# An expert layer on Trainium2: GpSimd's gathers and scatters, from a loop with copied indices to written-out code

## The chip, the core and the metric

The kernel runs on one core of one Trainium2 chip. The metric is device time in microseconds (us); of the kernel before there are three runs, with a median of 521.87 us (520.72 to 522.24). One more execution was recorded by the hardware profiler; all durations below come from it.

## The reference, cut to what matters

4096 tokens of 192 channels (16 images of 16 x 16) go through a convolution block, an attention block and an expert block. Only the expert block is touched:

```
t = t + ffn(layernorm(t))
ffn(x):
    logits = einsum('btd,ed->bte', x, gate_w)         # 8 experts
    p, idx = top_k(softmax(logits), 2)                # 2 experts for each token
    p = p / (sum(p) + 1e-8)
    h = silu(x @ gate_bank[e]) * (x @ up_bank[e])     # 192 -> 384
    y = h @ down_bank[e]                              # 384 -> 192
    return sum over the two chosen e of p[e] * y[e]
```

The kernel computes only the chosen experts.

## The kernel before, in words

Four phases follow one another, each a block of programs, one for each engine, with a barrier between blocks: convolution, attention, routing and experts. Routing sorts the 8192 pairs of a token and an expert by expert, and cuts them into 72 tiles of 128 rows, so that a tile has one expert. It leaves `idx_map` in on-chip memory: for each tile and each of 128 partitions two integers, the token's row to be gathered (entry 0) and the row to be scattered to (entry 1). `tile_exp` holds each tile's expert. VectorE writes both, in the routing block.

In the expert block (`expert_phase`, from L1023), the engines work on the tiles 0 to 71 in one order:

- GpSimd starts the indirect transfers. `gather` (L1057) brings a tile's 128 rows of `rows` (256 channels and 8 gates) from device memory into `xt`, a ring of XR = 8 slots. `scatter` (L1067) writes a tile's results from `y`, a ring of YR = 4 slots, to `chosen_rows` in device memory. A gather first copies the tile's two indices from `idx_map` into a ring of 8 slots `idx` (L1060), waits for its own copy (L1061) and names the slot in `idx` as the transfer's offsets (L1063). The scatter of the same tile uses the other index of that slot (L1072). `landed` (L1076) waits until the scatter of two tiles ago has arrived, because the slot in `idx` that it read is then written again. Six gathers are started ahead (AHEAD = 6); then for each tile j come scatter(j), landed(j - 2) and gather(j + 6). The first eight tiles and the last eight are written out, the 56 between run in a loop of 7 rounds with 8 tiles in each (L1089), in which tile number, waited values and places in `idx_map` come from registers.
- TensorE turns the rows (`turn_x`, L1115 and L1116, after a wait for the gather), multiplies by the gate and the up matrices (`product`, L1124 to L1128), turns the hidden values (`turn_h`, L1135) and multiplies by the down matrix (`down_product`, L1143 to L1152). In step r it does gate(r), turn_x(r + 1), turn_h(r - 1), up(r), down(r - 2). Its steps are a loop of eight at a time (L1187).
- ScalarE copies out of accumulation memory and applies silu, and scales a tile's result with its gate (`weigh`, L1219, which reads `xt`). VectorE makes the low parts and the product with the silu, and adds the two halves of a result into `y` (`add_parts`, L1283, after a wait that the scatter of four tiles ago has arrived).
- SyncE waits for all scatters (L1333), then loads the two results of each token, VectorE adds them to the tokens, and SyncE stores.

Gathers and scatters use one queue. A tile's scatter waits for `y_done`, which VectorE counts up at the end of `add_parts`.

Of the kernel before, what the change touches and what calls it, by code (L numbers as in the profile page):

```python
# [18 lines left out]
I32 = mybir.dt.int32  # L19
# [4 lines left out]
P = 128  # L24
# [16 lines left out]
RING = 2  # L41
XR = 8
AHEAD = XR - 2
YR = 4
# [18 lines left out]
def made(n):  # L63

    return n + 1 + RING
# [15 lines left out]
def program(nc, x, xT, w1, w2, lowpass, wqkv, cos, sin, gate, wgu, down, tri, ident, iotas, ytab, out):  # L81
# [6 lines left out]
    with ExitStack() as whole:  # L88
# [29 lines left out]
        attention_phase(nc, xs, mean, rstd, eye, wqa, wqb, cos_t, sin_t, ga, gb, rows, row_tiles, down, wd, lg)  # L118
        routing_phase(nc, lg, tri, iotas, row_tiles, idx_map, tile_exp)
        expert_phase(nc, xs, eye, rows, chosen_rows, out, wa_hi, wa_lo, wb_hi, wb_lo, wd, idx_map, tile_exp)  # L120


# [900 lines left out]
def expert_phase(nc, xs, eye, rows, chosen_rows, out, wa_hi, wa_lo, wb_hi, wb_lo, wd, idx_map, tile_exp):  # L1023

    with ExitStack() as stack:
        a = Scope(nc, stack, "moe")
        xt = a.sb("xt", [P, XR, ROW])
        idx = a.sb("idx", [P, XR, 2], I32)

        x_hi = a.sb("x_hi", [P, RING, 2 * P], F32R)  # L1030
        x_lo = a.sb("x_lo", [P, RING, P], F32R)
# [2 lines left out]
        yy, y = a.sb("yy", [P, RING, 2, C]), a.sb("y", [P, YR, C])  # L1034
# [6 lines left out]
        gathered = [a.sem(f"gathered{s}") for s in range(XR)]  # L1041
        scattered = [a.sem(f"scattered{s}") for s in range(YR)]
        picked, out_stored = ([a.sem(f"{n}{s}") for s in range(PR)] for n in ("picked", "out_stored"))
        sum_done, total_done = a.sem("sum_done"), a.sem("total_done")
        idx_done, pool_turn = a.sem("idx_done"), a.sem("pool_turn")
        xt_done, gate_done, up_done, ht_done, y_mm = (a.sem(n) for n in ("xt_done", "gate_done", "up_done", "ht_done", "y_mm"))
        x_hi_done, x_lo_done, x_lob_done = a.sem("x_hi_done"), a.sem("x_lo_done"), a.sem("x_lob_done")
        silu_done, hid_done, weighed = a.sem("silu_done"), a.sem("hid_done"), a.sem("weighed")
# [1 line left out]
        N = TILES_MAX  # L1050

        with nc.Block() as block:
            @block.gpsimd
            def _(pool):
                pool.sem_inc(idx_done, RING)

                def gather(i, r):  # L1057

                    j, n, slot = XR * i + r, i + r // XR, r % XR
                    nc.gpsimd.tensor_copy(idx[:, slot, :], idx_map[:, bass.ds(j, 1), :]).then_inc(idx_done, 1)  # L1060
                    pool.wait_ge(idx_done, made(j))  # L1061
                    pool.sem_inc(pool_turn, 1)
                    nc.gpsimd.indirect_dma_start(  # L1063
                        xt[:, slot, :], None, rows.ap(),
                        bass.IndirectOffsetOnAxis(ap=idx[:, slot, 0:1], axis=0)).then_inc(gathered[slot], 16)

                def scatter(i, r):  # L1067

                    j, slot = XR * i + r, r % XR
                    pool.wait_ge(y_done, made(j))  # L1070
                    pool.sem_inc(pool_turn, 1)
                    nc.gpsimd.indirect_dma_start(  # L1072
                        chosen_rows.ap(), bass.IndirectOffsetOnAxis(ap=idx[:, slot, 1:2], axis=0),
                        y[:, slot % YR, :], None).then_inc(scattered[slot % YR], 16)

                def landed(i, r):  # L1076

                    pool.wait_ge(scattered[r % YR], 16 * (XR // YR * i + r // YR) + 16)
                    pool.sem_inc(pool_turn, 1)


                for r in range(AHEAD):
                    gather(0, r)
                for r in range(XR):
                    scatter(0, r)
                    if r >= 2:
                        landed(0, r - 2)
                    gather(0, r + AHEAD)
                with pool.Fori(1, N // XR - 1) as i:  # L1089
                    for r in range(XR):  # L1090
                        scatter(i, r)
                        landed(i, r - 2)
                        gather(i, r + AHEAD)
                n = N // XR - 1
                for r in range(XR):
                    scatter(n, r)
                    landed(n, r - 2)
                    if r < 2:
                        gather(n, r + AHEAD)

            @block.tensor
            def _(pe):
# [318 lines left out]
```

## Time and profile before

| | |
|---|---|
| median of 3 runs | 521.87 us |
| profiled execution | 525.97 us, span 524.2 us |
| mean granted TensorE clock | 0.853 |
| expert block | from 236.2 us to the end |
| gathers | 72, mean 1016 ns each on GpSimd |
| scatters | 72, mean 991 ns |
| copies of indices | 72, mean 195 ns |

The span is the time from the first to the last instruction. An indirect transfer's time on GpSimd is the time in which the engine prepares it; the data move later. The number in brackets behind a row of the timeline is how long the engine sat idle ahead of the instruction, and what ended that ("issue": nothing that the profile shows). "PEld" are TensorE's weight loads, which run ahead of its matmuls; since a matmul's end is modelled, an idle time shows more plainly in them. Weight loads that wait, in a row, do so for the wait that stands ahead of the first of them.

### The profile page before, as it was taken

How to read it: one execution, taken by the hardware profiler on the slowest of the kernel's cores; microseconds unless marked ns; L12 is line 12 of the kernel's file. 1: busy time of each engine (PE TensorE's matmuls, PEld its weight loads, DVE VectorE, ACT ScalarE, POOL GpSimd, SP SyncE). 2: the span in 40 equal slices, each digit the busy share in tenths (PEclk: the TensorE clock that was granted, in tenths of full speed). 3: DMA queues.
4: the chain of work that ended last, by engine and by line, in shares of the span. 5: the costliest groups of instructions: out<-in, count | busy, mean ns of one | idle time of the engine just before them, and what ended most of it. 6: DMA issues, size and time to landing. Idle time of an engine off the chain costs nothing.

```text
span 524.2 us, 9292 instructions
## 1 busy us (share of the span) xinstructions
PE 406.2 (77%) x2236; PEld 369.8 (71%) x2237; DVE 309.0 (59%) x764; ACT 207.4 (40%) x481; POOL 242.1 (46%) x353
## 2 busy tenths in 40 slices
PE   5799928468897473385999999999999998999100
PEld 5699827467786462384989999999999997999100
DVE  2266672787875727991655655566655555555164
ACT  3443503413323110472545555555555554555100
POOL 0155542455554510005366666666666665665200
PEclk9999999787757555555999999999999999999655
DMA  7988510022222121101122222222222222222498
GB/s 209 245 200 227 138 57 0 24 63 63 63 63 64 41 80 35 11 1 52 38 73 71 71 72 70 65 71 71 69 67 69 69 71 60 67 70 62 131 352 268
DMA packets 47391, 47.07 MB, mean 90 GB/s; under 512 B 14313, under 2 KB 40332, under 8 KB 47372
## 3 DMA queue, kind: packets, MB, share of 16 engines
q1 hardware_dynamic: 40460, 30.04, 20.8%
q0 software_dynamic: 6912, 16.82, 11.0%
q8 instruction: 7, 0.11, 0.1%
q14 instruction: 12, 0.10, 0.1%
HBM read 32.16 MB, written 14.68 MB: 89 GB/s over the span
## 4 chain that ended last, share of the span: by engine, by line
PE 42%; DMA 5%; issue 3%; SPq 2%; POOL 1%; DVE 1%; ACT 0%; POOLq 0%; ACTq 0%; DVEq 0%
PE moe_ps_y L1149 8%; PE moe_ps_h L1135 4%; PE moe_ps_x L1115 3%; DMA wa_hi<-chosen_rows 3%; PE moe_ps_gt L1124 2%; PE moe_ps_u L1124 2%; PE moe_ps_u L1125 2%; PE moe_ps_u L1127 2%; PE moe_ps_u L1128 2%; PE moe_ps_u L1126 2%; PE moe_ps_gt L1125 2%; PE moe_ps_gt L1126 2%; PE moe_ps_y L1151 2%; PE moe_ps_gt L1128 2%; PE moe_ps_gt L1127 2%
## 5 line engine op out<-in xcount | busy, mean ns | idle before, releaser
L1063 POOL DMA_INDIRECT moe_xt<-rows,moe_idx x72 | 73.1, 1016 | 61.5 <-POOL moe_idx L1060 25.6
L1072 POOL DMA_INDIRECT chosen_rows<-moe_y,moe_idx x72 | 71.4, 991 | 34.4 <-issue 20.3
L1149 PE MATMUL moe_ps_y<-wd,moe_h_hi 128*128 x216 | 72.5, 361 | 1.3 <-DVE moe_h_lo L1280 0.6
L1225 ACT ACTIVATE moe_yy<-moe_ps_y,moe_xt 128x384 f32<-128x384 f32 x72 | 41.9, 582 | 75.5 <-PE moe_ps_y L1149 74.5
L1288 DVE TENSOR_TENSOR moe_y<-moe_yy 128x192 f32<-128x192 f32 x72 | 25.9, 360 | 60.9 <-ACT moe_yy L1225 57.2
L1205 ACT ACTIVATE moe_x_hi<-moe_ps_x 128x256 fp32r<-128x256 f32 x72 | 27.7, 385 | 50.1 <-PE moe_ps_x L1116 48.6
L1264 DVE TENSOR_TENSOR moe_x_lo<-moe_ps_x,moe_x_hi 128x128 fp32r<-128x128 f32 x72 | 21.0, 292 | 44.5 <-issue 27.6
L1149 PEld LDWEIGHTS moe_ps_y<-wd,moe_h_hi 128*128 128x128 f32 x216 | 40.8, 189 | 5.4 <-issue 4.9
L1280 DVE TENSOR_TENSOR moe_h_lo<-moe_ps_h,moe_h_hi 128x384 fp32r<-128x384 f32 x72 | 40.2, 558 | 2.7 <-ACT moe_h_hi L1217 0.5
L1274 DVE TENSOR_TENSOR moe_hid<-moe_ps_u,moe_sg 128x384 f32<-128x384 f32 x72 | 39.5, 548 | 1.2 <-ACT moe_sg L1211 1.2
L1151 PE MATMUL moe_ps_y<-wd,moe_h_lo 128*128 x144 | 36.1, 251 | 0.0
L1217 ACT ACTIVATE moe_h_hi<-moe_ps_h 128x384 fp32r<-128x384 f32 x72 | 35.5, 493 | 0.5 <-PE moe_ps_h L1135 0.5
L1135 PE MATMUL moe_ps_h<-eye,moe_hid 128*128 128x128 f32 x216 | 35.4, 273 | 0.0
L1211 ACT ACTIVATE moe_sg<-moe_ps_gt 128x384 f32<-128x384 f32 x72 | 34.9, 485 | 0.0
L1060 POOL COPY moe_idx<-idx_map 128x2 int32 (+1 forms) x72 | 14.1, 195 | 37.2 <-POOLq L857 37.0
L480 PE MATMUL attn_ps_a<-eye,attn_xn 128*128 128x128 f32 x32 | 12.3, 393 | 24.4 <-DVE attn_xn L472 23.2
L1124 PE MATMUL moe_ps_u<-wa_hi,moe_x_hi 128*128 x72 | 30.6, 425 | 0.0
L765 DVE TENSOR_TENSOR attn_prod<-attn_qkv,attn_kk 128x384 f32<-128x384 f32 x16 | 17.7, 1141 | 21.9 <-POOL attn_kk L701 21.9
L1115 PE MATMUL moe_ps_x<-eye,moe_xt 128*128 128x128 f32 x72 | 22.7, 315 | 10.0 <-DMA moe_xt<-rows,moe_idx 9.8
L350 POOL TENSOR_TENSOR wa_lo<-conv_stage,wa_hi 128x768 f32 (+1 forms) x8 | 15.1, 1888 | 32.6 <-ACT wb_hi L319 32.6
L238 PE MATMUL conv_ps_w<-conv_w1a,conv_xta 128*128 128x48 f32 x64 | 20.2, 416 | 9.2 <-DMA conv_xtb<-in_xT 9.2
L1151 PEld LDWEIGHTS moe_ps_y<-wd,moe_h_lo 128*128 128x128 f32 x144 | 27.3, 190 | 0.0
(185 smaller groups left out, 1173.0 us busy)
## 6 DMA issues: line engine op xcount, KB each, us to landing
wa_hi<-chosen_rows SPq DMA_DIRECT2D x16, 384.0 KB, 6.2
xs<-in_x SPq DMA_DIRECT2D x8, 384.0 KB, 6.0
conv_stage<-in_wgu SPq DMA_DIRECT2D x8, 384.0 KB, 3.8
conv_stage<-in_wgu SPq DMA_DIRECT2D x16, 192.0 KB, 4.7
rows<-attn_xr SPq DMA_DIRECT2D x8, 384.0 KB, 2.7
out<-xs SPq DMA_DIRECT2D x8, 384.0 KB, 6.2
attn_stage<-in_down SPq DMA_DIRECT2D x8, 288.0 KB, 3.3
conv_xta<-in_xT SPq DMA_DIRECT2D x8, 256.0 KB, 4.2
```

The lines of the kernel that those rows point to most:

```text
L1063: nc.gpsimd.indirect_dma_start(xt[:, slot, :], None, rows.ap(), bass.IndirectOffsetOnAxis(ap=idx[:, slot, 0:1], axis=0)).then_inc(gathered ...
L1072: nc.gpsimd.indirect_dma_start(chosen_rows.ap(), bass.IndirectOffsetOnAxis(ap=idx[:, slot, 1:2], axis=0), y[:, slot % YR, :], None).then_i ...
L1115: nc.tensor.transpose(ps_x[:, 0:P], xt[:, slot, 0:P], eye[:])
L1124: nc.tensor.matmul(at, x_hi[:, s, 0:P], wa_hi[:, e, w], start=True, stop=False)
L1135: ins = nc.tensor.transpose(ps_h[:, bass.ts(k, P)], hid[:, s, bass.ts(k, P)], eye[:])
L1149: ins = nc.tensor.matmul(both, hi, halves, start=(k == 0), stop=(k == 2))
L1151: nc.tensor.matmul(first, lo, high, start=False, stop=False)
L1211: nc.scalar.activation(sg[:, s, :], ps_g[:, s, 0:HID], ACT.Silu).then_inc(silu_done, 1)
L1217: nc.scalar.activation(h_hi[:, s, :], ps_h[:, 0:HID], ACT.Copy).then_inc(h_hi_done, 1)
L1225: nc.scalar.activation(yy[:, s].rearrange("p h c -> p (h c)"), ps_y[:, s, 0:2 * C], ACT.Copy, scale=xt[:, slot, bass.ds(GC + e, 1)]).then_ ...
L1274: nc.vector.tensor_tensor(hid[:, s, :], ps_u[:, s, 0:HID], sg[:, s, :], ALU.mult).then_inc(hid_done, 1)
L1280: nc.vector.tensor_tensor(h_lo[:, s, :], ps_h[:, 0:HID], h_hi[:, s, :].bitcast(F32), ALU.subtract).then_inc(h_lo_done, 1)
```

## The change

GpSimd's program is written out over all 72 tiles with constants; the gather takes its offsets from `idx_map[:, j, 0:1]` and the scatter from `idx_map[:, j, 1:2]`; the ring `idx`, its copies, the waits for the copies and `landed` are gone. The order of gathers and scatters is the same, and so are all other engines' programs.

```diff
-        idx = a.sb("idx", [P, XR, 2], I32)
...
-                pool.sem_inc(idx_done, RING)
-
-                def gather(i, r):
-
-                    j, n, slot = XR * i + r, i + r // XR, r % XR
-                    nc.gpsimd.tensor_copy(idx[:, slot, :], idx_map[:, bass.ds(j, 1), :]).then_inc(idx_done, 1)
-                    pool.wait_ge(idx_done, made(j))
+
+                def gather(j):
+
+                    slot = j % XR
                     pool.sem_inc(pool_turn, 1)
                     nc.gpsimd.indirect_dma_start(
                         xt[:, slot, :], None, rows.ap(),
-                        bass.IndirectOffsetOnAxis(ap=idx[:, slot, 0:1], axis=0)).then_inc(gathered[slot], 16)
-
-                def scatter(i, r):
-
-                    j, slot = XR * i + r, r % XR
+                        bass.IndirectOffsetOnAxis(ap=idx_map[:, j, 0:1], axis=0)).then_inc(gathered[slot], 16)
+
+                def scatter(j):
+
                     pool.wait_ge(y_done, made(j))
                     pool.sem_inc(pool_turn, 1)
                     nc.gpsimd.indirect_dma_start(
-                        chosen_rows.ap(), bass.IndirectOffsetOnAxis(ap=idx[:, slot, 1:2], axis=0),
-                        y[:, slot % YR, :], None).then_inc(scattered[slot % YR], 16)
-
-                def landed(i, r):
-
-                    pool.wait_ge(scattered[r % YR], 16 * (XR // YR * i + r // YR) + 16)
-                    pool.sem_inc(pool_turn, 1)
...
+                        chosen_rows.ap(), bass.IndirectOffsetOnAxis(ap=idx_map[:, j, 1:2], axis=0),
+                        y[:, j % YR, :], None).then_inc(scattered[j % YR], 16)
+
+                for j in range(AHEAD):
+                    gather(j)
+                for j in range(N):
+                    scatter(j)
+                    if j + AHEAD < N:
+                        gather(j + AHEAD)
```

The lines left out at the second mark are the written-out beginning, the loop `with pool.Fori(1, N // XR - 1)` and the written-out end, which go.

## Rows read from the trace of the kernel before

**Rows 1.** The page, part 1: busy us (share of the span) and instructions of each engine.

```profile
PE 406.2 (77%) x2236; PEld 369.8 (71%) x2237; DVE 309.0 (59%) x764; ACT 207.4 (40%) x481; POOL 242.1 (46%) x353
```

**Rows 2.** Stretches: length, busy us (instructions) of each engine, clock, DMA share, GB/s.

```profile
240.60:252.00 11.40, 10.04 (x45) 8.71 (x45) 4.15 (x12) 4.94 (x10) 4.76 (x9) 0.70 0.22 59
375.00:400.00 25.00, 24.88 (x160) 23.01 (x159) 15.35 (x39) 13.28 (x30) 16.80 (x23) 1.00 0.24 69
492.00:524.20 32.20, 0.00 (x0) 0.00 (x0) 15.34 (x16) 0.00 (x0) 0.00 (x0) 0.50 0.91 293
```

**Rows 3.** Waits of TensorE's weight loads, 236 to 500 us: total, times, longest.

```profile
PEld moe_ps_x L1115 <- DMA moe_xt<-rows,moe_idx: 22.4, 48, 6.6
```

**Rows 4.** Timeline of GpSimd: start, us, engine, line, tiles [idle before, releaser].

```profile
424.52 1.00 POOL L1063 DMA_INDIRECT moe_xt<-rows,moe_idx  x1 [0.82 <-DVE moe_y L1288]
425.82 0.99 POOL L1072 DMA_INDIRECT chosen_rows<-moe_y,moe_idx  x1 [0.30 <-issue]
426.82 0.19 POOL L1060 COPY moe_idx<-idx_map 128x2 int32 x1
427.83 1.00 POOL L1063 DMA_INDIRECT moe_xt<-rows,moe_idx  x1 [0.82 <-DVE moe_y L1288]
429.14 0.99 POOL L1072 DMA_INDIRECT chosen_rows<-moe_y,moe_idx  x1 [0.30 <-issue]
```

**Rows 5.** Timeline of TensorE and VectorE around the same tiles.

```profile
424.03 0.33 PE L1115 MATMUL moe_ps_x<-eye,moe_xt 128*128 128x128 f32 x1
...
427.45 0.33 PE L1115 MATMUL moe_ps_x<-eye,moe_xt 128*128 128x128 f32 x1
...
427.38 0.36 DVE L1288 TENSOR_TENSOR moe_y<-moe_yy 128x192 f32<-128x192 f32 x1 [0.79 <-ACT moe_yy L1225]
```

**Rows 6.** Timeline of TensorE, early in the experts.

```profile
253.75 0.27 PE L1115 MATMUL moe_ps_x<-eye,moe_xt 128*128 128x128 f32 x1
...
256.89 0.27 PE L1115 MATMUL moe_ps_x<-eye,moe_xt 128*128 128x128 f32 x1
...
269.78 0.34 PE L1128 MATMUL moe_ps_gt<-wb_lo,moe_x_hi 128*128 x1
271.26 0.33 PE L1115 MATMUL moe_ps_x<-eye,moe_xt 128*128 128x128 f32 x1 [1.14 <-DMA moe_xt<-rows,moe_idx]
```

**Rows 7.** Timeline, end of the experts.

```profile
479.56 0.33 PE L1115 MATMUL moe_ps_x<-eye,moe_xt 128*128 128x128 f32 x1
...
485.84 0.36 DVE L1288 TENSOR_TENSOR moe_y<-moe_yy 128x192 f32<-128x192 f32 x1 [1.01 <-ACT moe_yy L1225]
...
487.01 0.97 POOL L1072 DMA_INDIRECT chosen_rows<-moe_y,moe_idx  x1 [1.97 <-DVE moe_y L1288]
```

**Rows 8.** Timeline of TensorE where its loop jumps back.

```profile
305.32 0.34 PE L1128 MATMUL moe_ps_u<-wb_lo,moe_x_hi 128*128 x1
305.81 0.44 PE L1149 MATMUL moe_ps_y<-wd,moe_h_hi 128*128 x1
```

**Rows 9.** Timeline of GpSimd, gather of tile 9.

```profile
267.20 1.00 POOL L1063 DMA_INDIRECT moe_xt<-rows,moe_idx  x1 [0.82 <-POOL moe_idx L1060]
```

**Rows 10.** DMA queues from 268 to 272 us: packets, MB, share of 16 engines.

```profile
q8 instruction: 1, 0.02, 1.8%
```

**Rows 11.** Timeline of GpSimd, gather of tile 59.

```profile
433.44 0.19 POOL L1060 COPY moe_idx<-idx_map 128x2 int32 x1
436.86 1.00 POOL L1063 DMA_INDIRECT moe_xt<-rows,moe_idx  x1 [3.22 <-issue]
```

**Rows 12.** DMA queues from 430 to 440 us.

```profile
q0 software_dynamic: 233, 0.58, 18.7%
```

**Rows 13.** Groups of GpSimd's instructions from 236 to 436 us.

```profile
L1063 POOL DMA_INDIRECT moe_xt<-rows,moe_idx x59 | 60.0, 1017 | 48.5 <-DVE moe_y L1288 20.5 <-POOL moe_idx L1060 19.8 <-issue 8.2
L1072 POOL DMA_INDIRECT chosen_rows<-moe_y,moe_idx x54 | 53.6, 993 | 23.4 <-issue 16.0 <-DVE moe_y L1288 7.4
```

**Rows 14.** Timeline of GpSimd, first gather.

```profile
237.42 1.23 POOL L1063 DMA_INDIRECT moe_xt<-rows,moe_idx  x1 [0.99 <-POOL moe_idx L1060]
```

More of the change, by code:

```diff
@@ L1044, in expert_phase @@
         sum_done, total_done = a.sem("sum_done"), a.sem("total_done")
-        idx_done, pool_turn = a.sem("idx_done"), a.sem("pool_turn")
+        pool_turn = a.sem("pool_turn")
         xt_done, gate_done, up_done, ht_done, y_mm = (a.sem(n) for n in ("xt_done", "gate_done", "up_done", "ht_done", "y_mm"))
@@ L1072, in scatter @@
                     nc.gpsimd.indirect_dma_start(
-                        chosen_rows.ap(), bass.IndirectOffsetOnAxis(ap=idx[:, slot, 1:2], axis=0),
-                        y[:, slot % YR, :], None).then_inc(scattered[slot % YR], 16)
-                def landed(i, r):
-                    pool.wait_ge(scattered[r % YR], 16 * (XR // YR * i + r // YR) + 16)
-                    pool.sem_inc(pool_turn, 1)
[L1082 to L1099, printed above, removed]
+                        chosen_rows.ap(), bass.IndirectOffsetOnAxis(ap=idx_map[:, j, 1:2], axis=0),
[6 more added lines that the diff above has]
+                        gather(j + AHEAD)
             @block.tensor
```

## The prediction, made before the changed kernel was timed

> **What bounds the kernel now.** I read the busy shares first [rows 1]: TensorE is busy for 77% of the span, no other engine above 59%, and GpSimd, which only starts transfers in the experts, shows 46%. A share says little, so I went to stretches [rows 2]. From 375 to 400 us TensorE is busy 24.88 of 25.00 us at a granted clock of 1.00, which would say "TensorE bound, leave GpSimd alone". But a matmul's end is modelled, so small gaps vanish in that figure. The weight loads show them: they wait 22.4 us in 48 places for gathered rows, 6.6 us of it ahead of the first tile [rows 3]. So the reader should compare paces, not shares. From tile 5 to tile 71 a tile costs TensorE 222.67 / 66 = 3.37 us [rows 6, 7], and its turning of rows starts 2.93 us after the gather it needs was started (424.52 to 427.45) [rows 4, 5].
>
> GpSimd's own pace is made of one gather, one scatter and one copy of indices: 1.00 + 0.30 + 0.99 + 0.01 + 0.19 + 0.82 = 3.31 us, and that is the distance of its gathers (424.52 to 427.83) [rows 4]. The 0.30 us stands before a scatter whose wait was long met; the 0.82 us stands before each gather, which waits for the copy ahead of it. It never idles for work in this part: the result that a scatter needs (tile 52's sum ends at 427.38 + 0.36 = 427.74) is there 1.40 us before the scatter starts at 429.14 [rows 4, 5]. When nothing is late TensorE needs less: the first turn of tile 4 starts at 253.75, of tile 5 at 256.89 and all in between runs without a gap, 3.14 us [rows 6]. So in the expert loop TensorE (3.14 to 3.15) is paced by GpSimd (3.31), and this is the bound that the change touches.
>
> **The change part by part.**
>
> Copy of indices and its wait (removed, 72 times). Per tile this takes 0.19 + 0.82 + 0.01 us off GpSimd and puts one ordinary gap between scatter and gather. The nearest row for a transfer right behind another one is the 0.30 us [rows 4]; bounds are 0 and the 0.82 us of a gather behind a copy. I take 0.30, since the wait that makes 0.82 is gone. GpSimd then needs 1.00 + 0.30 + 0.99 + 0.30 = 2.6 us per tile if nothing is awaited, well under 3.15.
>
> Wait for landed scatters (removed). It guarded the copied indices. On the rows it costs nothing (the copy starts 0.01 us behind the scatter [rows 4]), so I count 0 both ways.
>
> Loop turned into written-out code with constants. No register work and no jump back. What it costs in instruction fetches the trace cannot show directly; I bound it by 0 and by one visible hole of the size of the 1.31 us at 269.78 [rows 6] for each of about three blocks, 4 us together, and take 0. The Trainium skill (Runtime: NRT & Kernel Launch, section Instruction fetch mechanics) says that straight code is streamed ahead in blocks while the engine works, and that taken branches break this. By that rule the written-out program costs nothing; this trace has no long written-out program on GpSimd that would show it, and the sum does not use it.
>
> What becomes late next: a serial chain over three tiles. Turn of tile n+3 leads to tile n's sum, 3.71 us later (424.03 to 427.74) [rows 5]; the scatter then really waits, and a scatter that waited starts 0.81 us after its sum (485.84 + 0.36 = 486.20 to 487.01) [rows 7]; it takes 0.99, gap 0.30, and the gather's rows are turned 2.93 us after its start [rows 4, 5]. 3.71 + 0.81 + 0.99 + 0.30 + 2.93 = 8.74 us for three tiles, 2.91 per tile. That is under 3.15, so TensorE sets the pace, with about 0.7 us of slack per three tiles. Even with 0.82 in place of 0.30 it is 9.26, or 3.09.
>
> The sum, over the stretch from the turn of tile 5 (256.89) to that of tile 71 (479.56), now 222.67 us [rows 6, 7]:
> - 66 tiles at 3.15: 207.9.
> - Where TensorE's own loop jumps back it has a hole: 305.32 to 305.81 is 0.49 where 0.17 is usual, with 0.08 lost right behind, so 0.40; eight of these, the first one smaller, I count at 0.36 each: 2.9 [rows 8]. The bounds are 0 (GpSimd's lateness alone made it) and 0.40.
> - The hole at 269.78 (1.48 instead of 0.17) is put down to gather 9, but that gather needs 4.06 us (267.20 to 271.26) where the others need 2.8 to 2.95, and there is instruction traffic on the DMA engines between 268 and 272 us [rows 6, 9, 10]. I take it as not made by GpSimd's pace and keep it: 1.3 (bounds 0 and 1.3).
> - The gather of tile 59 starts 3.23 us after its copy (433.63 to 436.86) instead of 0.82, once in the kernel, and GpSimd's own queue is the only one with traffic from 430 to 440 us [rows 11, 12]. It is the 114th indirect transfer: 59 gathers and 54 scatters are ahead [rows 13]. The order and the number of transfers stay the same, so I keep its excess, 2.41 us, behind scatter 53. On the chain above: 8.74 + 2.41 = 11.15 against 9.45 for three tiles, a hole of 1.7 in TensorE (bounds 0, and 2.4 with no slack left).
> Together 207.9 + 2.9 + 1.3 + 1.7 = 213.8, that is 8.9 us less.
>
> The start: the first gather starts at 237.42, 0.99 us behind its copy of 0.19 us, the first work of the block (236.24) [rows 14], and TensorE waits for nothing else. Without the copy it can start about 0.81 us [rows 7] behind the barrier that the copy followed, and that I put at 236.1: near 236.9, a gain of 0.5. Bounds: 0.2 and 1.2 (start at once). The tiles behind it are on TensorE, at the lower granted clock (0.70 over the stretch of 240.6 to 252 [rows 2]), and have their rows in time already, so nothing more comes there.
>
> The tail stays: from the last turn (479.56) on, GpSimd starts scatters 0.8 us behind their sums, then 32 us of loads, sums and stores follow in which GpSimd does nothing, with the DMA engines 91% busy [rows 2, 7]. It moves forward as it is.
>
> Gain 8.9 + 0.5 = 9.4 us. The profiled execution took 525.97 us with a span of 524.2 us; I expect a span near 514.8. The median of the runs is 521.87, 4.1 below the profiled one; I carry the gain over whole: 521.87 - 9.4 = 512.5 us. About 0.3%, 1.6 us, is what a measurement here can tell from no change.
>
> **The rivals.**
> 1. Nothing remains of the three kept holes (clear run): TensorE never waits for a gather and its loop hole shrinks. Gain 9.4 + 1.3 + 1.7 + 1 to 2 = 13.4 to 14.4, so 508. For it: the 1.3 us hole does end with a gather. Against it: the loop hole stands between two matmuls that need no gather [rows 8]. Chance 0.10.
> 2. A smaller gain. Either the written-out code is fetched late (up to three holes of 1.3 us, 4 us), or the runs without a profiler are 4.1 us quicker than the profiled one because just GpSimd's pace was slower under the profiler; then about half of what I take away was never there. Either gives 521.87 - 9.4 + 4 = 516.5. For it: GpSimd's part is made of many small sequencer steps. Against it: TensorE's holes for gathers are regular over 200 us. Chance 0.18.
> 3. Slower: the fixed cost ahead of an indirect transfer isn't the wait for the copy but the transfer's own. Then two transfers back to back have 0.82 us before each one, GpSimd's pace becomes 1.00 + 0.82 + 0.99 + 0.82 = 3.63 us, and 66 tiles lose 66 x (3.63 - 222.67/66) = 17 us: 539. It decides at the point where both gaps together pass 1.32 us (3.31 - 1.99). Against it: the 0.30 us before every scatter that did not wait. Chance 0.04.
> 4. The bound is the chain and not TensorE: gathers land late once they follow 1.3 us instead of 2.0 us behind a scatter. With the 4.06 us of gather 9 for each, three tiles take 9.87 us, 3.29 per tile, and the kernel gains only 66 x (3.37 - 3.29) = 5 less the two stalls that stay, 2 to 3 us; with a little more delay, nothing: 519 to 522. Against it: scatter and gather would still not start together. Chance 0.06.
> That the written-out program orders the transfers in another way is excluded: it starts the same gathers and scatters in the same order.
>
> **How the numbers follow.** The forecast, TensorE's pace, has 0.62, with its own range of 510.0 to 515.0 (loop hole 0 to 0.40, start 0.2 to 1.2, the two stalls). The clear run has 0.10, the smaller gain 0.18, the chain 0.06 and slower 0.04. The range takes in rival 2 and nearly rival 1: 508.5 to 517.5. Faster by over 0.3% (under 520.3): forecast, rivals 1 and 2 and a part of 4, 0.90; within 0.3%: half of rival 4 and some unseen cover, 0.06; slower: 0.04.
>
> **What would show it.** Right: no gap of 0.82 us on GpSimd but before scatters, which now wait for the sum; the gather right behind at 0.30; distances of turns of 3.15 us with 3.5 us at each eighth; TensorE's weight loads waiting for gathers in a few places instead of 48; one long gap at gather 59; the last turn near 470. Wrong: a gap near 0.8 before every gather (rival 3), gathers that need over 3.6 us (rival 4), or holes with instruction packets beside them (rival 2). If turns of rows still come at 3.3 us without waiting for a gather, the forecast's reading of 3.14 as TensorE's own pace is wrong.

## The result

The changed kernel takes 509.28 us (median of 4 runs, 509.05 to 509.66) against 521.30 us of the kernel before (520.56 to 522.24): a ratio of 0.9744 [0.9713, 0.9774], 12.0 us less. The forecast was 9.4 us less, 512.5. GpSimd's pace gave way to TensorE's as forecast, and the gain is 2.6 us larger: 509.28 lies under the forecast's own range of 510.0 to 515.0, though within the wider one of 508.5 to 517.5.

The page of the changed kernel, its span, busy times and GpSimd's two groups (line, engine, operation, tiles, count | busy us, mean ns | idle us ahead of them and what ended it):

```profile
span 507.7 us, 8980 instructions
PE 393.6 (78%) x2236; PEld 371.1 (73%) x2237; DVE 309.1 (61%) x764; ACT 207.7 (41%) x481; POOL 224.8 (44%) x281
L1067 POOL DMA_INDIRECT chosen_rows<-moe_y,idx_map x72 | 71.2, 988 | 76.1 <-DVE moe_y L1265 74.2
L1059 POOL DMA_INDIRECT moe_xt<-rows,idx_map x72 | 70.1, 974 | 61.1 <-issue 58.8
```

Beside [rows 1] little seems to have happened: TensorE stands at 78% instead of 77%. What changed is who waits. GpSimd's scatters now stood 74.2 us waiting for VectorE's sums. The stretch of 375 to 400 us says the same, with its length, busy us (instructions) of PE, PEld, DVE, ACT, POOL, clock, DMA share and GB/s:

```profile
375.00:400.00 25.00, 25.00 (x169) 24.72 (x168) 15.49 (x41) 14.28 (x32) 15.44 (x17) 1.00 0.26 75
```

TensorE was "busy" 24.88 of 25.00 us before [rows 2] and is 25.00 now, half a per cent more, yet 169 matmuls stand in the stretch instead of 160. The weight loads show it better: 23.01 before, 24.72 now. Their waits for gathered rows over the experts (us, times, longest) fell from 22.4 us in 48 places [rows 3] to three places, the first of them the unavoidable one ahead of tile 0:

```profile
PEld moe_ps_x L1092 <- DMA moe_xt<-rows,idx_map: 7.5, 3, 6.2
```

GpSimd in the steady state, for comparison with [rows 4] (start, us, engine, line, tiles [idle before, releaser]):

```profile
233.79 1.23 POOL L1059 DMA_INDIRECT moe_xt<-rows,idx_map  x1 [37.77 <-issue]
...
407.19 0.97 POOL L1059 DMA_INDIRECT moe_xt<-rows,idx_map  x1 [0.30 <-issue]
409.04 0.99 POOL L1067 DMA_INDIRECT chosen_rows<-moe_y,idx_map  x1 [0.88 <-DVE moe_y L1265]
410.33 0.97 POOL L1059 DMA_INDIRECT moe_xt<-rows,idx_map  x1 [0.30 <-issue]
...
418.49 0.99 POOL L1067 DMA_INDIRECT chosen_rows<-moe_y,idx_map  x1 [0.90 <-DVE moe_y L1265]
421.45 0.98 POOL L1059 DMA_INDIRECT moe_xt<-rows,idx_map  x1 [1.97 <-DVE moe_y L1265]
422.73 0.99 POOL L1067 DMA_INDIRECT chosen_rows<-moe_y,idx_map  x1 [0.30 <-issue]
```

VectorE's sums, the first of which the scatter at 409.04 needs:

```profile
407.86 0.36 DVE L1265 TENSOR_TENSOR moe_y<-moe_yy 128x192 f32<-128x192 f32 x1 [0.79 <-ACT moe_yy L1202]
...
414.15 0.36 DVE L1265 TENSOR_TENSOR moe_y<-moe_yy 128x192 f32<-128x192 f32 x1 [0.80 <-ACT moe_yy L1202]
```

The first ends at 408.22 and the scatter starts 0.82 us later; the gather follows at 0.30. GpSimd's gathers are 3.14 us apart (407.19 to 410.33) where they were 3.31 apart: TensorE now sets the pace, as the turns of rows show on TensorE:

```profile
253.13 0.27 PE L1092 MATMUL moe_ps_x<-eye,moe_xt 128*128 128x128 f32 x1
256.27 0.27 PE L1092 MATMUL moe_ps_x<-eye,moe_xt 128*128 128x128 f32 x1
...
301.71 0.34 PE L1105 MATMUL moe_ps_u<-wb_lo,moe_x_hi 128*128 x1
301.88 0.34 PE L1126 MATMUL moe_ps_y<-wd,moe_h_hi 128*128 x1
...
407.71 0.27 PE L1092 MATMUL moe_ps_x<-eye,moe_xt 128*128 128x128 f32 x1
410.85 0.27 PE L1092 MATMUL moe_ps_x<-eye,moe_xt 128*128 128x128 f32 x1
...
423.30 0.34 PE L1105 MATMUL moe_ps_gt<-wb_lo,moe_x_hi 128*128 x1
424.32 0.33 PE L1092 MATMUL moe_ps_x<-eye,moe_xt 128*128 128x128 f32 x1 [0.68 <-DMA moe_xt<-rows,idx_map]
...
425.63 0.33 PE L1105 MATMUL moe_ps_u<-wb_lo,moe_x_hi 128*128 x1
426.07 0.44 PE L1126 MATMUL moe_ps_y<-wd,moe_h_hi 128*128 x1
...
462.86 0.27 PE L1092 MATMUL moe_ps_x<-eye,moe_xt 128*128 128x128 f32 x1
```

From tile 5 to tile 71 the turns take 462.86 - 253.13 = 209.73 us; before it was 222.67 [rows 6, 7], and 222.09 in a second profile of the kernel before. So the loop gave 12.4 to 12.9 us. From 301.71 to 301.88, in the round of TensorE's loop that [rows 8] show, there is no hole any more (0.17; before 0.49). At tile 59 there still is one (424.32, 1.02 us behind the matmul ahead instead of 0.17), and right behind it, from 425.63 to 426.07, the loop's hole is back at 0.44. It is the only one of the seven rounds in this stretch that has it.

The place of this hole has to be put right. [rows 8] and the prediction have it where the loop jumps back. But it stands between up(18) and down(16), in the middle of the first step of a round of eight, 2.8 us behind that round's first matmul (gate(18), at 303.05 us in the profile of before), and at the jump itself, ahead of 303.05, matmuls follow each other at 0.20 us. What is special there can be read in the program (`steps`): in the first two steps of a round it loads two experts' numbers into registers between up and down, in the others at most one. From up to down all fourteen profiles show 0.17 or 0.18 us in every other step; what is longer stands in these two. The profiler records no register loads, so that they make the hole is an inference. Below, "loop hole" means this one.

The two spans differ by more, 524.2 - 507.7 = 16.5 us, but 3.3 us of that lies in the blocks that nobody touched: the barrier ahead of the experts came at 236.1 in the profile of before, at 232.8 here, and at 232.6 in the second profile of before, whose span is 518.9. The start gave 0.3 us: the first gather comes 0.99 us behind the barrier (232.8 to 233.79) instead of 1.3. The time behind the last turn is the same within 1.5 us (before 44.6 and 43.5, after 44.8).

### The profile page after: what moved, and what is told of

It is laid out like the page before. It is cut to its first block, busy times and chain, and to the rows that moved or that the text cites. A ratio compares the mean times of both kernels' runs of the same rounds, so it can differ in the third digit from the quotient of the medians.

```text
span 507.7 us, 8980 instructions
## 1 busy us (share of the span) xinstructions
PE 393.6 (78%) x2236; PEld 371.1 (73%) x2237; DVE 309.1 (61%) x764; ACT 207.7 (41%) x481; POOL 224.8 (44%) x281
## 3 DMA queue, kind: packets, MB, share of 16 engines
q0 software_dynamic: 6912, 16.82, 11.2%
## 4 chain that ended last, share of the span: by engine, by line
PE 44%; DMA 4%; SPq 2%; issue 2%; DVE 1%; POOL 0%; ACT 0%; POOLq 0%; DVEq 0%; ACTq 0%
PE moe_ps_y L1126 8%; PE moe_ps_h L1112 4%; PE moe_ps_gt L1101 3%; DMA wa_hi<-chosen_rows 3%; PE moe_ps_u L1101 2%; PE moe_ps_u L1102 2%; PE moe_ps_u L1105 2%; PE moe_ps_u L1103 2%; PE moe_ps_gt L1102 2%; PE moe_ps_u L1104 2%; PE moe_ps_gt L1105 2%; PE moe_ps_gt L1103 2%; PE moe_ps_gt L1104 2%; PE moe_ps_y L1128 2%; SPq L1315 2%; PE moe_ps_x L1092 2%
## 5 line engine op out<-in xcount | busy, mean ns | idle before, releaser
L1067 POOL DMA_INDIRECT chosen_rows<-moe_y,idx_map x72 | 71.2, 988 | 76.1 <-DVE moe_y L1265 74.2
L1059 POOL DMA_INDIRECT moe_xt<-rows,idx_map x72 | 70.1, 974 | 61.1 <-issue 58.8
L1126 PE MATMUL moe_ps_y<-wd,moe_h_hi 128*128 x216 | 70.9, 353 | 0.7 <-DVE moe_h_lo L1257 0.5
L1101 PE MATMUL moe_ps_gt<-wa_hi,moe_x_hi 128*128 x72 | 24.9, 346 | 1.3 <-DVE moe_x_hi L1244 1.3
L480 PEld LDWEIGHTS attn_ps_a<-eye,attn_xn 128*128 128x128 f32 x32 | 6.4, 199 | 26.8 <-issue 17.9
```

The lines of the kernel that those rows point to most:

```text
L1059: nc.gpsimd.indirect_dma_start(xt[:, slot, :], None, rows.ap(), bass.IndirectOffsetOnAxis(ap=idx_map[:, j, 0:1], axis=0)).then_inc(gathere ...
L1067: nc.gpsimd.indirect_dma_start(chosen_rows.ap(), bass.IndirectOffsetOnAxis(ap=idx_map[:, j, 1:2], axis=0), y[:, j % YR, :], None).then_inc ...
L1101: nc.tensor.matmul(at, x_hi[:, s, 0:P], wa_hi[:, e, w], start=True, stop=False)
L1126: ins = nc.tensor.matmul(both, hi, halves, start=(k == 0), stop=(k == 2))
```

## The experiments

Every kernel ran beside the kernel before, on the same chip; three chips were used (e7 and e9 on one, e10 and e11 on another, all others on a third). "Distance" is that of undisturbed turns of rows in us, "waits" those of TensorE's weight loads for gathers.

| kernel | median, us | ratio to before | distance | waits, us / places |
|---|---|---|---|---|
| b_again: before | 523.44 | 1.0003 [0.9972, 1.0035] | 3.31 | 21.8 / 47 |
| a_again: after | 508.99 | 0.9735 [0.9688, 0.9783] | 3.155 | 7.1 / 2 |
| e1_written_out | 522.18 | 1.0000 [0.9971, 1.0028] | 3.31 | 21.6 / 46 |
| e2_early_copy | 510.35 | 0.9757 [0.9718, 0.9797] | 3.155 | 8.4 / 3 |
| e3_copy_wait | 522.61 | 1.0008 [0.9978, 1.0037] | 3.31 | 21.8 / 48 |
| e4_copies2 | 510.68 | 0.9755 [0.9705, 0.9804] | 3.17 | 8.9 / 4 |
| e5_copies6 | 516.19 | 0.9864 [0.9808, 0.992] | 3.17 to 3.4 | 12.6 / 18 |
| e6_copy_wait_ahead8 | 516.49 | 0.9849 [0.9792, 0.9905] | 3.15, then 3.31 | 14.2 / 24 |
| e7_ahead8 | 515.05 | 0.9856 [0.9821, 0.989] | 3.15 | 6.1 / 1 |
| e11_ahead8_again | 506.46 | 0.9688 [0.9636, 0.974] | 3.155 | 6.2 / 1 |
| e10_ahead7 | 507.33 | 0.9714 [0.9673, 0.9755] | 3.155 | 6.2 / 1 |
| e9_ten_more | 529.43 | 1.0145 [1.0096, 1.0193] | 3.16 | 7.8 / 5 |

**b_again and a_again** are the two kernels unchanged, for a second profile of each.

> The kernel before, unchanged, for a second profile. Its first profiled execution took 525.97 us, 4.7 over the median of 521.3, and the barrier ahead of the experts came about 3 us later than in the kernel after, where nothing was changed. Theory (that execution was an unusually long one, ahead of the experts and in two stalls): a span near 519.5 to 521, the first gather near 234.5, the expert loop from the turn of tile 5 to that of tile 71 between 221 and 223 us. Rival (the change moves the earlier blocks too): the first gather again at 237.4 and a span of 524. Time ratio 1.000.

The span is 518.9 us and the loop took 222.09 us, so the first profile (524.2) was an unusually long execution, ahead of the experts above all. The hole behind gather 9 (1.48 us [rows 6]) came again but smaller (0.92). The long wait ahead of gather 59 came again in full (3.22 us at 432.71), so it belongs to the program.

> The kernel after, unchanged, beside its variants on the same chip, and for a second profile. Ratio 0.973 to 0.978; expert loop from the turn of tile 5 to that of tile 71 at 209.7 us again, one long gap ahead of gather 59 that costs TensorE 1.3 us.

With a span of 507.1 and a loop of 209.44 us it is the kernel after again, with the long gap ahead of gather 59 and the one loop hole behind it (0.45 us at 426.4).

**e1_written_out: only the loop is undone.** GpSimd's program is written out with constants, but the copies, their waits and the waits for landed scatters stay.

```diff
-                    for r in range(XR):
-                        scatter(i, r)
-                        landed(i, r - 2)
-                        gather(i, r + AHEAD)
+                for j in range(N):
+                    scatter(j // XR, j % XR)
+                    if j >= 2:
+                        landed((j - 2) // XR, (j - 2) % XR)
+                    if j + AHEAD < N:
+                        gather((j + AHEAD) // XR, (j + AHEAD) % XR)
```

> GpSimd's program written out with constants as in the kernel after, but the copy, the wait for it and the wait for landed scatters are kept. Theory (the wait for the copy makes the pace): gathers stay 3.31 us apart, TensorE's turns too, ratio to before 0.996 to 1.000; only the longer round at each jump back of the loop (3.47 in place of 3.31) may go, 7 x 0.16 = 1.1 us. Rival (the loop and its register work made the pace): turns 3.15 us apart and a ratio near 0.976.

Its GpSimd timeline:

```profile
323.43 1.00 POOL L1063 DMA_INDIRECT moe_xt<-rows,moe_idx  x1 [0.82 <-POOL moe_idx L1060]
324.73 0.99 POOL L1072 DMA_INDIRECT chosen_rows<-moe_y,moe_idx  x1 [0.30 <-issue]
325.72 0.19 POOL L1060 COPY moe_idx<-idx_map 128x2 int32<-128x2 int32 x1
326.73 0.99 POOL L1063 DMA_INDIRECT moe_xt<-rows,moe_idx  x1 [0.82 <-POOL moe_idx L1060]
```

The 0.82 us and the 3.31 stay as in [rows 4], TensorE's loop hole stays (0.44 us), and the ratio is 1.000: loop or written-out text is worth nothing that these runs can tell (0.3% either way).

**e2_early_copy: only the wait is taken off the path.** This is the kernel before with its loop, copies and waits; each copy is made one tile earlier, so that the gather's wait for it has long been met (and `landed` waits for the scatter of the tile before).

```diff
-                        landed(i, r - 2)
+                        landed(i, r - 1)
+                        copy(i, r + AHEAD + 1)
                         gather(i, r + AHEAD)
```

> The kernel before with loop, registers, copies and landed waits kept, but each copy is made one tile earlier, behind the scatter and ahead of the gather of the tile before, so that the gather's wait for its copy is long met. Theory: the gap ahead of a gather falls from 0.82 to about 0.30, GpSimd needs 1.00 + 0.30 + 0.99 + 0.19 + 0.30 = 2.8 us per tile and TensorE sets the pace at 3.15: ratio 0.976 to 0.981, nearly all of the gain. Rival (loop and registers): no change, ratio 0.998 to 1.002. A third way: the sequencer handles loop code slower than the engine works, gathers near 3.2 apart, ratio about 0.99.

Its GpSimd timeline:

```profile
322.92 0.19 POOL L1060 COPY moe_idx<-idx_map 128x2 int32 x1
323.26 0.99 POOL L1067 DMA_INDIRECT moe_xt<-rows,moe_idx  x1 [0.15 <-issue]
...
326.06 0.19 POOL L1060 COPY moe_idx<-idx_map 128x2 int32 x1
326.41 0.99 POOL L1067 DMA_INDIRECT moe_xt<-rows,moe_idx  x1 [0.15 <-issue]
```

The gap is 0.15 instead of 0.82 and the gathers are 3.15 us apart. TensorE's loop hole is gone but for the one behind the late gather 59 (0.44 us at 427.6), and all but about a microsecond of the change's gain is there. The work of 72 copies remains; only the wait for one that was just issued is gone.

**e3_copy_wait: the wait alone is put back.** The kernel after, plus one copy and a wait for it ahead of each gather; nothing reads the copy.

```diff
                     slot = j % XR
+                    nc.gpsimd.tensor_copy(idx[:, j, 0], idx_map[:, j]).then_inc(idx_done, 1)
+                    pool.wait_ge(idx_done, j + 1)
```

> The kernel after, with one copy of the tile's two indices put back ahead of each gather and a wait for it; nothing reads the copy. Theory: gathers are 3.31 us apart again and the ratio to before is 0.994 to 1.000; TensorE's hole of 0.3 to 0.4 us where its loop jumps back, which the kernel after does not have, comes back, if it is lateness of gathers that exposes it. Rival (the ring of copied indices or the landed waits were the cost): the ratio stays at 0.976. Second rival for the hole (it was made by GpSimd's loop jump): it stays away, though the pace is 3.31.

The GpSimd timeline of this kernel:

```profile
325.51 0.19 POOL L1059 COPY moe_idx<-idx_map 128x2 int32<-128x2 int32 x1
326.52 0.99 POOL L1062 DMA_INDIRECT moe_xt<-rows,idx_map  x1 [0.82 <-POOL moe_idx L1059]
```

And TensorE at its loop hole:

```profile
300.77 0.34 PE L1108 MATMUL moe_ps_u<-wb_lo,moe_x_hi 128*128 x1
301.22 0.44 PE L1129 MATMUL moe_ps_y<-wd,moe_h_hi 128*128 x1
```

The whole gain is lost (1.0008), and with the late gathers TensorE's loop hole is back in every round (0.45 instead of 0.17), though TensorE's program is untouched. e1 and e3 have late gathers throughout and the hole in six and in seven of seven rounds; e2 and after have one late gather that falls into such a step, 59, and the hole in that round alone. So the loop's code makes the hole only while TensorE is held up just ahead of it; e6 will show both in one kernel.

**e4_copies2 and e5_copies6: GpSimd's work without a wait.** The kernel after, plus two or six copies ahead of each gather that nobody awaits.

```diff
                     slot = j % XR
+                    for k in range(2):      # e5: range(6)
+                        nc.gpsimd.tensor_copy(idx[:, j, k], idx_map[:, j])
```

> The kernel after, with two copies of the tile's indices put ahead of each gather that nobody waits for and nobody reads. A copy is 0.19 us and a gather right behind a copy whose wait was long met had a gap of 0.15, so GpSimd gets 2 x 0.19 + 0.15 - 0.30 = 0.23 us more per tile: pace 2.8, chain over three tiles 8.69 + 0.23 = 8.92, both under TensorE's 9.47. Theory (waits and total pace count, the copy's own time does not): turns 3.155 us apart, ratio to before 0.975 as the kernel after, gathers started 3.3 ahead of their turn in place of 3.5. Rival (each microsecond on GpSimd comes back in the time): 66 x 0.23 = 15 us more, ratio 1.00.

> The kernel after, with six such copies ahead of each gather. Theory of pace (one scatter, six copies and one gather in series): 1.00 + 0.30 + 0.99 + 6 x 0.195 + 0.15 = 3.61 us per tile, against 3.155; 66 x 0.455 = 30 us more than the kernel after, ratio to before 1.03. Rival, the chain from the turn over the sum and the scatter to the gather, with three tiles to run in: (8.69 + 1.02) / 3 = 3.24 us per tile, 6 us more, ratio 0.987. TensorE's hole at its jump back is there again in both.

Two copies cost 1.7 us beside a_again, which is not clear of noise, and not the rival's 15. The turns show a distance of 3.17 instead of 3.155 (about 1 us in all, cause open) and a hole of 0.9 us at tile 9. GpSimd was early enough there; the gather itself was slow and landed 4.5 us after its start, where gather 9 of after took 2.8. The gather's start and the weight load that waited for it:

```profile
262.13 1.00 POOL L1062 DMA_INDIRECT moe_xt<-rows,idx_map  x1 [0.15 <-issue]
266.66 0.14 PEld L1095 LDWEIGHTS moe_ps_x<-eye,moe_xt 128*128 128x128 f32 x1 [1.06 <-DMA moe_xt<-rows,idx_map]
```

Six copies gave this on GpSimd:

```profile
361.27 1.00 POOL L1062 DMA_INDIRECT moe_xt<-rows,idx_map  x1 [0.15 <-issue]
362.57 0.99 POOL L1070 DMA_INDIRECT chosen_rows<-moe_y,idx_map  x1 [0.30 <-issue]
363.56 0.78 POOL L1060 COPY moe_idx<-idx_map 128x2 int32<-128x2 int32 x6
364.49 1.00 POOL L1062 DMA_INDIRECT moe_xt<-rows,idx_map  x1 [0.15 <-issue]
```

Six queued copies take 0.78 us together and not 6 x 0.19 = 1.14, so the expectation's price for them was too high, in its theory (ratio 1.03) and in its rival (0.987). The rival's number was met (0.9864) by luck: the scatters shown don't wait for a sum (0.30, "issue"), so the chain isn't the bound. The pace is 1.00 + 0.30 + 0.99 + 0.78 + 0.15 = 3.22 us, which is what the rows show (361.27 to 364.49). Over 66 tiles that is 66 x (3.22 - 3.155) = 4.3 us plus holes, and the kernel is some 7 us longer than a_again (516.19 and 508.99). So between 2.7 us of GpSimd (e4) and 3.22 (e5) lies TensorE's 3.155, the point from which GpSimd's time counts. The loop hole follows: e5 has it (0.42 to 0.46 us) in every round from the second on, e4 only behind gather 59.

**e6_copy_wait_ahead8: a deeper lead under a slow GpSimd.** e3 with gathers started 8 tiles ahead instead of 6.

```diff
-AHEAD = XR - 2
+AHEAD = XR
```

> The kernel after with the copy and the wait for it, as in e3, but with 8 gathers ahead in place of 6, so that a gather is started two tiles earlier. Theory of pace: GpSimd still needs 3.31 us per tile; the lead of two tiles is used up at 0.16 us per tile after about 40 tiles, so turns are 3.155 apart at first and 3.31 apart from about tile 45 on; with the long gap ahead of one gather it is used up somewhat earlier. Gain over e3 about 6 to 7 us, ratio to before 0.985 to 0.990. Rival of latency (a gather only came too late after its scatter): all of it is gained, turns 3.155 apart to the end, ratio 0.973.

Weight loads that waited for gathers, from 232 to 360 us (which holds only the first tile's wait) and from 400 to 480:

```profile
PEld moe_ps_x L1095 <- DMA moe_xt<-rows,idx_map: 6.5, 1, 6.5
...
PEld moe_ps_x L1095 <- DMA moe_xt<-rows,idx_map: 6.3, 17, 2.1
```

Turns are 3.15 us apart until about tile 44, while the lead of gather over turn shrinks from 9.3 us (tile 8) to 2.84 (tile 46); then they are 3.31 apart. That is a faster consumer eating up a buffer: 3.31 is a rate of GpSimd's, not a delay that a deeper ring removes for good. The loop hole comes in the same moment. Here it is in the last round with lead and in the next one:

```profile
376.97 0.34 PE L1108 MATMUL moe_ps_u<-wb_lo,moe_x_hi 128*128 x1
377.15 0.37 PE L1129 MATMUL moe_ps_y<-wd,moe_h_hi 128*128 x1
...
403.18 0.34 PE L1108 MATMUL moe_ps_u<-wb_lo,moe_x_hi 128*128 x1
403.65 0.43 PE L1129 MATMUL moe_ps_y<-wd,moe_h_hi 128*128 x1
```

One program, one execution: 0.18 us with lead, 0.47 without.

**e7_ahead8, e10_ahead7, e11_ahead8_again: a deeper lead under the fast GpSimd.** The kernel after with gathers 8 ahead (e7, and the same kernel again as e11) or 7 ahead (e10, `AHEAD = XR - 1`), to take away the stall at gather 59.

> The kernel after with 8 gathers ahead in place of 6 (the sum of tile j is there before its scatter, so the slot of tile j in xt is free for gather j + 8). Expected: gathers wait two tiles longer for their turn, the long gap ahead of the 114th transfer, now gather 60 (8 gathers, then scatter k is transfer 9 + 2k and gather 8 + k is transfer 10 + 2k), no longer reaches TensorE, and the loop is 1.3 to 1.6 us shorter than the kernel after: 208.2 us from the turn of tile 5 to that of tile 71, ratio to before 0.972. Rival (the hole at tile 59 isn't lateness of the gather): it stays, ratio as the kernel after.

> The kernel after with 7 gathers ahead in place of 6. With 8 the time was 6 us longer than the kernel after though no turn of rows waited for a gather: ScalarE stood still for up to 3.6 us with nothing in the trace to wait for, first while GpSimd started five transfers back to back behind its one long gap. Theory A (the lead as such is harmless, 7 is enough to hide the long gap ahead of the 114th transfer): the turns are 3.155 us apart to the end and the ratio to before is 0.970 to 0.973, a little better than the kernel after. Theory B (each gather more in flight or in the opening row costs): halfway, ratio about 0.979, with the same standstills of ScalarE behind the long gap.

> The kernel with 8 gathers ahead, unchanged, for a second profile. If its standstills belong to the program, they are at the same tiles again (ScalarE ahead of its copies of tiles 55 and 62, TensorE's turns 60, 62, 65 and 69 over 3.6 us apart) and the ratio to before is 0.985 again. If they came by chance in that execution, they stand elsewhere and the ratio may fall to 0.972.

GpSimd in e10, where the long gap now stands ahead of scatter 53, and then in e11, where it stands ahead of gather 60:

```profile
415.18 0.99 POOL L1067 DMA_INDIRECT chosen_rows<-moe_y,idx_map  x1 [0.89 <-DVE moe_y L1265]
416.47 0.97 POOL L1059 DMA_INDIRECT moe_xt<-rows,idx_map  x1 [0.30 <-issue]
420.76 1.00 POOL L1067 DMA_INDIRECT chosen_rows<-moe_y,idx_map  x1 [3.32 <-DVE moe_y L1265]
```

```profile
418.45 0.98 POOL L1059 DMA_INDIRECT moe_xt<-rows,idx_map  x1 [1.97 <-DVE moe_y L1265]
```

The gap stayed (2.43 us over the usual 0.89 ahead of a scatter in e10, 1.67 over the usual 0.30 ahead of a gather in e11), but no turn waits for it: waits fall to the first tile's 6.2 us, and tile 5 to tile 71 takes 66 x 3.155 = 208.2 us, 1.5 less than after. e11's 506.46 us (505.68 to 507.79) is the fastest of all kernels here, with a ratio of 0.9688; its interval overlaps a_again's, so it is the traces, not the times, that show the 1.5 us.

The same program as e11 took 515.05 us as e7, on another chip, though the kernel before is as fast on either (522.21 and 522.16). No turn waits for a gather there either. Instead ScalarE stands still, and no engine of the core is named as what released it. Its timeline:

```profile
425.40 0.49 ACT L1188 ACTIVATE moe_sg<-moe_ps_gt 128x384 f32<-128x384 f32 x1
429.49 0.58 ACT L1202 ACTIVATE moe_yy<-moe_ps_y,moe_xt 128x384 f32<-128x384 f32 x1 [3.60 <-remote]
```

This happens just when GpSimd, catching up behind the long gap, starts transfers back to back (five from 422.24 to 427.38), and the turns of tiles 60, 62, 65 and 69 come 3.7 to 4.9 us apart. In e11 the same catching up does no harm.

**e9_ten_more: does the long gap go by the count of transfers?** The kernel after, with ten gathers of 8 numbers per row and a wait for them between the first six gathers and the first scatter. If it does, the gap moves from gather 59 to gather 54.

```diff
+                for k in range(10):
+                    nc.gpsimd.indirect_dma_start(
+                        spare[:, k, :], None, rows.ap(),
+                        bass.IndirectOffsetOnAxis(ap=idx_map[:, k, 0:1], axis=0)).then_inc(spare_in, 16)
+                pool.wait_ge(spare_in, 160)
```

> The kernel after with ten more gathers of 8 numbers in each row, behind the first six, into a tile that nobody reads, and a wait for them. The one long gap on GpSimd stood ahead of gather 59 in all profiles so far, the 114th indirect transfer. Theory (it comes by the count of transfers): now gather 54 is the 114th (16 gathers, then gather 6 + k is transfer 18 + 2k) and the gap stands ahead of it. Rival (by tile, by data or by bytes moved): it stays at gather 59, or moves by another number. Second rival (by the time since the start): it stays near 419 us. If it comes by the count, the time is that of the kernel after plus whatever the ten cost at the start, up to 3 us.

GpSimd:

```profile
447.66 0.97 POOL L1060 DMA_INDIRECT moe_xt<-rows,idx_map  x1 [1.96 <-DVE moe_y L1271]
```

The gap moved the other way, to gather 62, the 130th transfer. It had stood ahead of the 114th in every other kernel (gather 59, in e10 scatter 53, in e7 and e11 gather 60). Among the kernels with 144 transfers it goes by their number and not by tile or time (it ended between 418 and 437 us). With ten small ones ahead it came six transfers later than in them even if the ten are left out, so the number alone isn't the rule, and both rivals of the expectation are as wrong as its theory. The kernel was also some 20 us longer than after would be (1.0145, two runs, against 0.9744, of 521 us), which nothing expected: during the row of 16 transfers back to back (233.96 to 253.97) ScalarE stood still again, here in its timeline:

```profile
245.72 0.49 ACT L1194 ACTIVATE moe_sg<-moe_ps_gt 128x384 f32<-128x384 f32 x1
256.63 0.38 ACT L1188 ACTIVATE moe_x_hi<-moe_ps_x 128x256 fp32r<-128x256 f32 x1 [10.41 <-remote]
```

TensorE stood 6.11 us in the same stretch, and tile 5 was turned 9 us later than in after. The other 11 us were lost in the loop (220.60 us from tile 5 to tile 71), where ScalarE stood 2.1 to 2.7 us six more times with "remote" as releaser, behind only three to five transfers that GpSimd had started close together. e9 ran on the chip of e7, and of all profiles only these two name "remote" for these engines.

## Why the prediction was right on the pace and wrong on the holes it kept

- **The bound** ("TensorE (3.14 to 3.15) is paced by GpSimd (3.31)"): right. e3 gives it all back, e2 gets it without removing a copy, e1 shows that the rest of the change is neutral, and e5 places the crossing between 2.7 and 3.22 us. The measured distance is 3.155: 208.2 for 66 tiles, 207.9 forecast.
- **Copy and wait; the gap of 0.30**: right (0.30 at 407.19 and 410.33). What costs is the wait for a copy just issued (0.82 against 0.15 in e2), not the copy.
- **Wait for landed scatters, and the written-out program, at nothing**: right. e1 has 1.000, and none of the holes of 1.3 us that rival 2 put on late fetches. It has two packets of instructions in its expert loop that the kernel before hasn't (at 328 and 400 us); beside the first TensorE waited 0.46 us for a gather, beside the second no longer than in its neighbours (0.28). The Trainium skill (Runtime: NRT & Kernel Launch, section Instruction fetch mechanics) agrees that straight code is streamed ahead.
- **The serial chain** (8.74 us forecast): a sum 3.66 us after the turn (410.85 to 414.15 + 0.36), then 0.82 + 0.99 + 0.30 + 2.87 = 8.64 us. The slack was forecast at 0.7 us per three tiles; measured, a gather starts 3.53 us ahead of its turn's weight load where 2.87 would do (tile 59, which waited), 0.66.
- **TensorE's loop hole, 2.9 us: wrong, and the step of the prediction that failed.** That step is "the loop hole stands between two matmuls that need no gather", read as a proof that the hole is TensorE's own. In after it is gone (0.18) in six of seven rounds and stands (0.44) only behind the late gather 59; e3 has it in all seven; the kernel before itself has none in the first step of the round behind the slow gather 9, when the next gathers were early again; in e6 it comes in the round in which the lead is used up. The bound "0 (GpSimd's lateness alone made it)" was nearly the true end. Also, only seven of the eight rounds counted lie in the stretch (the first hole, at 251.9 us, is ahead of tile 5), so the term was 2.5 by its own price. Why a hold-up shows ten matmuls later stays an inference: a TensorE that has just waited would have nothing queued while it loads the experts' numbers.
- **The hole at 269.78, 1.3 us: kept, and not there.** Its reason was right: the gather itself was slow, and that is not GpSimd's pace. e4 shows it with a fast GpSimd (gather 9 landed after 4.5 us, where 2.8 is usual), b_again and e1 with a slow one (3.8). In after, a_again, e2 and e3 gather 9 landed after 2.8 to 2.9 us, so there was nothing for the slack of 0.66 us to hide. What the prediction had wrong is that the hole belongs to the program; it comes in some executions, and that it stayed away in after is luck.
- **Stall at tile 59, 1.7 us**: measured 1.26, 0.85 up to the turn of tile 59 and 0.41 from there to that of tile 60, of which 0.27 is the loop hole. The term that was mis-sized is the gap's excess on GpSimd: 2.41 over 0.82 behind a copy's wait before, 1.67 over 0.30 now (1.97). 1.67 less the slack of 0.66 is 1.01, as the weight loads waited (1.00).
- **Tiles 70 and 71**: another 0.2 us that nothing forecast. Gather 70 landed after 3.8 us.
- **Start, 0.5 us**: 0.3, within the bounds (0.2 to 1.2).

213.8 - 2.9 - 1.3 - 0.4 + 0.3 (66 tiles) + 0.2 (tiles 70 and 71) = 209.7, as measured. So the two kept holes, 4.2 us, are the miss, one of them by a wrong mechanism and one by luck, and the result lies nearer to rival 1 (508) than to the forecast. **Rival 1**, at 0.10, was right for two of its three holes and wrong for tile 59. **Rival 2**: the gain of the timed runs (12.0) is as large as that of like profiles (518.9 to 507.7, 11.2), so neither of its causes took part. **Rival 3** is refuted by the 0.30 us. **Rival 4** by gathers that landed after 2.7 to 2.9 us though they follow their scatter by 1.3.

## What to carry to other kernels

Compare the pace of each engine in the loop, with its gaps, and not busy shares: an engine that was busy for 46% of the span set the time, since 0.82 us of every 3.31 was a wait for its own last instruction. Issue the thing awaited one step earlier, or don't await it: moving the copies one tile ahead was worth as much as removing all 72, within the noise. When a late producer is put right, regular holes elsewhere on the consumer, even between instructions that don't need the producer, should be counted to the lateness until shown otherwise. A single hole behind one slow transfer is another matter: look whether it is there in a second profile before it goes into a sum.

## What the runs showed of the hardware

- An indirect transfer of 128 rows occupies GpSimd for about 1 us (0.95 to 1.00 in the rows of after, 1.23 for the first). It starts 0.30 us behind another one, 0.15 behind an unawaited copy, and 0.8 to 0.9 behind a semaphore that was just counted up, GpSimd's own included.
- Small copies (128 x 2 numbers) overlap when queued: 0.19 us for one, 0.30 for two, 0.78 for six.
- A gather usually lands 2.7 to 2.9 us after its start. In the eleven profiles that give landings, 18 of the 772 gathers that have one (the first of each kernel left out) took 3.2 to 4.5 us, and during 17 of these a packet of instructions moved on the DMA engines. During 46 others one moved too and the gather was not slow. So the packet is nearly always there and isn't enough; that it causes the delay wasn't tried.
- Every kernel has one long gap ahead of an indirect transfer, the 114th of 144, or the 130th of 154 when ten small ones are ahead. With gathers 7 or 8 ahead and a fast GpSimd no turn waits for it. What it is stays open.
- TensorE's hole of about 0.3 us in the first or second step of a loop round comes only when it has just been held up (e6: 0.18 us with lead, 0.47 without).
- On one chip, ScalarE stood 3.60 and 10.41 us with "remote" as releaser while GpSimd issued transfers back to back, and 2.1 to 2.7 us six more times; the same program was 1.7% longer there than on another chip (515.05 and 506.46), the kernel before was not (522.21 and 522.16). Whether the chip or the occasion made it wasn't tried.
